# The skip term of a Mamba stack: u scaled by D in place on VectorE and added by TensorE transposes, instead of products with a diagonal matrix

## What is computed

```python
u = jax.nn.silu(jnp.transpose(xc, (0, 2, 1)))          # after the short convolution
dbl = u @ W_x
delta = jax.nn.softplus(dt @ W_dt + b_dt)
def step(h, inp):
    u_t, d_t, B_t, C_t = inp
    h = jnp.exp(d_t[..., None] * A) * h + (d_t * u_t)[..., None] * B_t[:, None, :]
    y = jnp.einsum('bds,bs->bd', h, C_t)
    return (h, y)
y = jnp.moveaxis(ys, 0, 1) + u * Dp                    # the skip term
y = y * jax.nn.silu(res)
return y @ W_out
```

## Time and profile before

| | |
|---|---|
| median of 3 runs | 2191.8 us (2189.04 to 2195.35) |
| profiled execution, its own time | 2192.7 us |
| its span, first to last instruction | 2190.9 us |
| TensorE busy | 94% of the span |
| VectorE, ScalarE, GpSimd busy | 68%, 66%, 68% |
| mean granted TensorE clock | 0.977 |

### The profile page before, as it was taken

How to read it: one execution, slowest core, us unless ns; L and a number is a source line. 1 busy time by engine, 2 the same in 40 slices (tenths; PEclk the granted TensorE clock), 3 DMA queues, 4 the chain that set the end, 5 groups by cost and what they waited for, 6 DMA issues and landing times.

```text
span 2190.9 us, 30857 instructions
## 1 busy us (share of the span) xinstructions
PE 2052.0 (94%) x11952; PEld 1444.5 (66%) x11952; DVE 1500.5 (68%) x1507; ACT 1450.1 (66%) x2294; POOL 1484.7 (68%) x845
## 2 busy tenths in 40 slices
PE   6989899999999999999999999999999889999997
PEld 3457677777777777777676777777777764444443
DVE  1268888888897989797879888887888970111201
ACT  0278888898887888888878888888788731000000
POOL 0039897989898888989897979798889960000000
PEclk9989999999999999999999999999999999989999
DMA  5211111111111112111111121111111410000000
GB/s 182 88 58 40 58 41 60 40 60 49 60 39 59 39 60 68 41 68 39 61 41 58 41 68 40 60 42 66 40 50 39 155 59 37 1 29 0 10 0 19
DMA packets 34137, 113.13 MB, mean 52 GB/s; under 512 B 6148, under 2 KB 8836, under 8 KB 33480
## 3 DMA queue, kind: packets, MB, share of 16 engines
q1 hardware_dynamic: 33992, 111.17, 14.9%
HBM read 95.95 MB, written 15.20 MB: 51 GB/s over the span
## 4 chain that ended last, share of the span: by engine, by line
PE 55%; DVE 15%; ACT 14%; issue 11%; POOL 4%; DMA 1%; SPq 0%; DVEq 0%; POOLq 0%; ACTq 0%
PE b_ps L1107 11%; PE y_all L1118 9%; DVE hid L855 8%; ACT hid L545 6%; ACT dub_t L558 5%; PE y_all L1216 5%; PE b_ps L1216 4%; DVE u L730 4%; PE bank_b L999 3%; POOL hid L418 3%; PE bank_a L1014 3%; PE y_all L919 3%; PE bank_b L1014 2%; PE bank_a L1023 2%; PE y_all L1229 2%
## 5 line engine op out<-in xcount | busy, mean ns | idle before, releaser
L855 DVE TENSOR_TENSOR_SCAN hid<-hid,b_ps 128x512 f32<-128x512 f32 x1024 | 1213.5, 1209 | 247.6 <-PE b_ps L1107 225.9
L418 POOL TENSOR_TENSOR hid<-hid,c_rep 128x1024 f32<-128x1024 f32 x512 | 1208.3, 2388 | 200.1 <-DVE hid L855 200.1
L1107 PEld LDWEIGHTS b_ps<-ident,dub_t 128*128 128x128 f32 x4096 | 481.8, 143 | 389.3 <-issue 220.1
L1107 PE MATMUL b_ps<-ident,dub_t 128*128 128x128 f32 x4096 | 637.8, 279 | 71.2 <-DVE hid L855 67.1
L545 ACT ACTIVATE hid<-delta,neg_a 128x512 f32<-128x512 f32 x1024 | 652.9, 711 | 0.4
L1118 PE MATMUL y_all<-ident,hid 128*128 128x128 f32 x4096 | 619.9, 275 | 7.3 <-POOL hid L418 6.3
L558 ACT ACTIVATE dub_t<-du_t,b_t 128x512 f32<-128x512 f32 x768 | 490.3, 712 | 58.9 <-PE b_ps L1107 57.2
L1118 PEld LDWEIGHTS y_all<-ident,hid 128*128 128x128 f32 x4096 | 484.1, 142 | 11.1 <-POOL hid L418 11.1
L409 POOL TENSOR_SCALAR dub_t<-du_t,b_t 128x512 f32<-128x512 f32 x256 | 174.7, 710 | 0.0
L730 DVE SCALAR_TENSOR_TENSOR u<-bank_b,conv_w_sb,u 128x511 f32<-128x511 f32 (+2 forms) x192 | 139.3, 725 | 0.7
L999 PE MATMUL bank_b<-xn,w_in_sb 128*128 128x512 f32 x256 | 132.1, 602 | 3.3 <-DVE u L730 3.3
(11 more groups left out here) (190 smaller groups left out, 1783.2 us busy)
## 6 DMA issues: line engine op xcount, KB each, us to landing
c_rep<-bc_dram SPq DMA_DIRECT2D x128, 512.0 KB, 3.7
hid<-x_t SPq DMA_DIRECT2D x4, 2048.0 KB, 8.7
x_dram<-x_out SPq DMA_DIRECT2D x16, 512.0 KB, 2.9
xt<-x_dram SPq DMA_DIRECT2D x15, 512.0 KB, 3.7
h_dram<-hid SPq DMA_DIRECT2D x4, 512.0 KB, 3.3
out<-y_d SPq DMA_DIRECT2D x4, 512.0 KB, 2.6
x_dram<-hid SPq DMA_DIRECT2D x3, 512.0 KB, 2.7
c_rep<-x_dram SPq DMA_DIRECT2D x3, 512.0 KB, 5.1
```

What stands on the lines that cost most here:

```text
L418: nc.gpsimd.tensor_tensor(part, part, c_rep[:, n % 2, s % GROUP, :].unsqueeze(1) .broadcast_to([P, HALF, SEQ]), ALU.mult).then_inc(hc_read ...
L855: nc.vector.tensor_tensor_scan(hid[:, i % RING, d, :], hid[:, i % RING, d, :], b_ps[d % 2][:, :], 0.0, ALU.mult, ALU.add)\
L1107: last = nc.tensor.transpose(b_ps[d % 2][:, c * P:(c + 1) * P], dub_t[:, i % DUB, c, d * P:(d + 1) * P], ident[:, :])
```

## The change

VectorE no longer makes diagonal matrices. In each step it multiplies block d of `u` by D in place (`scale_u`), at the slots of the new table `SCALE_U_AT`, after the scan of that slot. TensorE waits for that and adds the block with four transposes, in the form that `sum_states` has. Two of the four places in `SKIP_AT` move to later slots, and the two waits on `setup` go from 6 to 2.

```diff
-            diag_skip = sb("diag_skip", [P, NI, P])
+            scaled_u = sem("scaled_u")
...
-                    act.wait_ge(setup, 6)
+                    act.wait_ge(setup, 2)
...
-                    dve.wait_ge(ident_ready, 2)
-                    for d in range(NI):
-                        nc.vector.tensor_scalar(diag_skip[:, d, :], ident[:, :], vec_sb[:, 2, d:d + 1], None, ALU.mult)\
-                            .then_inc(setup, 1)
...
+                    def scale_u(k, d):
+                        dve.wait_ge(du_ready, 2 * k + d // HALF + 1)
+                        nc.vector.tensor_scalar(u[:, k % 2, d, :], u[:, k % 2, d, :], vec_sb[:, 2, d:d + 1], None, ALU.mult)\
+                            .then_inc(scaled_u, 1)
+
+                    SCALE_U_AT = {(3, 0): 0, (3, 1): 1, (3, 2): 2, (4, 1): 3}
...
+                                if live(k) and at in SCALE_U_AT:
+                                    scale_u(k, SCALE_U_AT[at])
...
                     def skip(k, d):
+                        pe.wait_ge(scaled_u, NI * k + d + 1)
                         for c in range(TC):
                             last = nc.tensor.matmul(y_ps[d][:, c * P:(c + 1) * P], u[:, k % 2, d, c * P:(c + 1) * P],
-                                                    diag_skip[:, d, :], start=False, stop=False, skip_group_check=True)
+                                                    ident[:, :], start=False, stop=False, is_transpose=True, skip_group_check=True)
                         last.then_inc(skip_done, 1)
...
-                    SKIP_AT = {(2, 1): 0, (2, 2): 1, (10, 0): 2, (10, 2): 3}
+                    SKIP_AT = {(5, 2): 0, (7, 3): 1, (10, 0): 2, (10, 2): 3}
...
-                                    pe.wait_ge(setup, 6)
+                                    pe.wait_ge(setup, 2)
```

## The result

| | before | changed |
|---|---|---|
| median | 2191.5 us (4 runs, 2189.0 to 2195.4) | 2223.6 us (4 runs, 2219.1 to 2230.9) |
| ratio to before | | 1.0148, 95% interval 1.0117 to 1.0180 |
| profiled execution, its span | 2192.7, 2190.9 us | 2224.2, 2222.4 us |
| mean granted TensorE clock | 0.977 | 0.964 |

The change costs 32 us. The forecast was 16, inside its range and on its side, but three quarters of the cost have a cause that the sum put at nothing: TensorE's clock. Ratios and intervals leave out executions more than 1.5% above the fastest of their kernel, three in experiment 1 and one in experiment 9.

What follows compares the result with a forecast made beforehand. The prediction took no single engine as the bound: the chain of waits changes engines a dozen times a step. Its terms, 6.2 + 4.9 + 1.3 + 4.5 - 0.8 = +16.1 us on 2192.7, gave about 2208, range 2187 to 2240.

Steps and rivals of the forecast that it cites:

- the 28.8 us taken from TensorE: 64 skip blocks, each 0.45 us shorter as transposes than as products; predicted to gain nothing, lying ahead of waits or under taps.
- The rival that TensorE's time counts: TensorE is the real bound, so its saved time is won: about 2163 us, or 2178 for half; chance 0.15.
- The block at (5, 2): Skip block moved into the stretch TensorE holds without a gap: +0.44 us per step, 6.2 us over steps 0 to 13.
- the cover: TensorE's 0.62 us wait for `y_copy` at (8, 2) was to absorb the 0.44 us block at (7, 3), costing nothing.
- The scalings against GpSimd: Scalings at (3, 0) to (4, 1) wait for running GpSimd products: 0.6 us each, 1.5 or more at (3, 2).
- a TensorE stall of 0.35 us: The late scan of (3, 3) was to hold up TensorE 0.35 us a step, 4.9 us over 14 steps.
- The rival of the lost races: GpSimd goes first at (3, 1) or (4, 1), stalling TensorE: 24 to 57 us, 2232 to 2265; chance 0.14.
- the rival that the scalings do not touch GpSimd: Scalings run without waiting for GpSimd, so the sum is +7.4 us: 2200 us; chance 0.2.
- Steps 14 and 15, and the diagonals: Step 14 +1.3 us on GpSimd, step 15 +4.5 on VectorE's scalings; no diagonals before the first step, -0.8.
- The clock: TensorE's slow stretches behind row sums and 16-column turns: one more or fewer, 5 us each side, nothing in the sum.
- the 1.8 us taken out of (2, 1) and (2, 2): Two skip blocks leave ahead of TensorE's wait for `gate` at (2, 3); the wait grows by 1.8 us, gain nothing.
- The rival of more slow stretches: Fewer products with weights let every step get a slow stretch: 13 more by 5.2 us, about 2275; chance 0.02.

Runs made afterwards that it cites:

- experiment 1: The changed kernel with its four skip blocks at (7, 3), (10, 0), (10, 2), (10, 3): 2217.1 us, ratio 1.0067 from its seven shortest runs of ten.
- experiment 9: The changed kernel with the row sums of squares taking 64 columns of ones instead of one: 2189.1 us, ratio 0.9982.
- experiment 4: The changed kernel without the scalings and TensorE's wait for them, so the factor D is left out: 2226.5 us, ratio 1.0147.
- experiment 5: The changed kernel with blocks 0 and 1 again as diagonal products at (2, 1) and (2, 2), only blocks 2 and 3 scaled: 2194.2 us, ratio 1.0006.
- experiment 6: experiment 1 plus eight faint products (1e-20 diagonal) at (2, 1) and (2, 2): 2196.4 us, ratio 1.0021.
- experiment 7: experiment 1 plus sixteen transposes of a faint 128x128 matrix at (2, 1) and (2, 2): 2195.0 us, ratio 1.0015.
- 12: experiment 1 with the row sums of squares taking 64 columns of ones instead of one: 2184.3 us, ratio 0.9959.
- experiments 3: The kernel before with two of block 1's four skip products moved from (2, 2) to (5, 2), no scalings: 2205.8 us, ratio 1.0058.
- 10: The changed kernel plus eight faint products (1e-20 diagonal) at (2, 1) and (2, 2): 2215.8 us, ratio 1.0097.
- experiment 8: The kernel before with the row sums of squares taking 64 columns of ones instead of one: 2176.1 us, ratio 0.9919.

## Why the prediction was right or wrong

**The bound, and the side.** Right. The chain changes engines often; the 28.8 us taken from TensorE bought nothing. The rival that TensorE's time counts fell at once: no step is below 102.5 us.

**The block at (5, 2).** Right to the hundredth. It was to add 0.44 us to every step, 6.2 in all; undisturbed steps are 0.45 us longer, 5.9 in all, and experiment 1 takes it away by moving the block. At (7, 3) the cover held: the wait for `y_copy` behind it shrank from 0.62 us to

```profile
1044.37 0.33 PE L1082 MATMUL bank_a<-ident,yg_t 128*128 128x128 f32 x1 [0.19 <-ACT y_d L527]
```

**The scalings against GpSimd.** The mechanism was right, the price was not. A one-input scaling does wait for a running GpSimd product, with the pattern of lengths worked out: short, short, long, slightly long (0.46, 0.46, 1.23 and 0.60 us). What the Trainium skill says (SBUF — State Buffer, Who interferes with whom), that a float32 `tensor_scalar` within SBUF and GpSimd lock each other out for whole instructions, the trace bears out with 1.23 us against 0.46. But the step that made a TensorE stall of 0.35 us of it, 4.9 us in all, failed: a free scaling is 0.46 us instead of 0.6, the waiting one 1.23 instead of 1.5 or more, and the two banks of `b_ps` took up what was left, a scan that starts 0.56 us later and is ready just in time. The stall did not occur, and by experiment 4 the scalings cost nothing in the steps. The rival of the lost races put its 24 to 57 us on a sum that held 4.9 of the same stall already; no scaling in an undisturbed step came near its 3 us. For the steps the rival that the scalings do not touch GpSimd had the right number for the wrong reason.

**Steps 14 and 15, and the diagonals.** 1.3 + 4.5 us were to come behind the last `dbl` copy; 2.8 did. Two of the four scalings of the last step waited, in the timeline of VectorE:

```profile
1739.26 1.89 DVE L744 TENSOR_SCALAR u<-u,vec_sb 128x512 f32<-128x512 f32 x1
...
1743.71 1.45 DVE L744 TENSOR_SCALAR u<-u,vec_sb 128x512 f32<-128x512 f32 x1
...
1753.47 1.61 DVE L761 TENSOR_TENSOR xt<-xt,xn 128x1024 f32<-128x1024 f32 x1
```

The last of these rows is the addition that took 5.80 us in the earlier trace rows: it now starts 1.9 us into the run of two GpSimd products instead of with it, and 4.2 us came back where the working had allowed for a part. That the place made the difference is argued, not tried. The comparison on eight columns, 4.32 us in the earlier trace rows, lost some of it again:

```profile
1792.22 6.76 DVE L786 TENSOR_TENSOR top<-logit 128x8 f32<-128x8 f32 x1
```

Both times it ends with a group of four GpSimd products (1767.4 before, 1798.95 after), and now it started earlier in it. The four scalings are 4.3 us together; 4.3 - 4.2 + 2.4 is 2.5 of the 2.8 us. So the scalings' own cost, 4.3 us here and 4.4 by experiment 4, was near the forecast's 5.8 for the two steps, and the sum missed what two other instructions would then wait less or more. Ahead of the first copy 1.7 us went, of which the diagonals' 0.8 is the part that was worked out; the rest, like the 4.4 us of the start-up, can be the clock there, and was not tried.

**The clock.** This is the step that failed. It was put as one slow stretch more or fewer, 5.2 us each (4.5 measured), and at nothing in the sum. It was 24 us, three quarters of the result: 19.9 in seven slow steps instead of three, 4.4 in the start-up, which may be chance. Two sentences of the prediction stood close to it. One costed the 1.8 us taken out of (2, 1) and (2, 2) at nothing, since the wait behind them takes them up. Their direct cost was nothing (experiment 5 against 1: the same undisturbed step), though what grew was less the wait for `gate` than two new ones for scans. But they were what kept TensorE fed at a place where it then waits, and without them that place starts slow stretches of its own (experiments 1, 6, 7, 12). The other saw that "small shifts" decide which step gets a stretch at the squares, and took them as noise. They are not only that. With the place full and steps of 102.98 us there are three long stretches, three or four steps apart (before, experiments 5, 6 and 7); with steps 0.45 us longer there are four and five, two or three steps apart (experiments 3 and 10); and widening the squares removed them all (experiments 8 and 9). How the length of a step sets that spacing, the runs don't show, and two lengths are too few for a rule. The rival of more slow stretches named the right effect with a chance of 0.02, and dismissed it by the earlier trace rows.

That dismissal was right in what it said. By the page's rule in the Trainium skill (TensorE: Matmul & The Clock Gate, PE-mode transpose) the 16 idle transposes of experiment 7 should have done nothing for the clock; they did the same as the products of experiment 6, 2195.0 against 2196.4 us. Transposes were not the trouble. Fewer microseconds of work were, and it made no difference which of these two kinds filled them. The kind did matter at the squares, where one-column products hold TensorE as long as wide ones and left its clock at 1.2 GHz behind them in three steps (experiment 8).

**The number.** Against 2192.7, the terms as measured in the two profiled executions are 5.9 for the steps (6.2 forecast), 0 for the stall (4.9), 2.8 behind the last copy (5.8), -1.7 ahead of the first (-0.8), and 24 for the clock (0): +31, where the forecast had +16. That the forecast lies in the right half of its range is in part luck: 8 us of terms that did not come stood in for clock that did, and the range reached to 2240 for lost races, of which there were none.

## What to carry to other kernels

Before taking work off TensorE ahead of a wait, look where its slow stretches begin and what the edit leaves at such places: an engine's time that "costs nothing" may be what keeps its clock up, and here 1.8 us a step were worth 8 us (intervals touching) in the changed kernel and 12 to 21 in experiment 1. Where a profile shows slow stretches behind a group of one-column products, widen them first; it costs no time and was worth 0.8% here, more than any move of work. And give a time that hangs on the pattern of slow stretches a wide range, since steps longer by 0.45 us in 103, with TensorE's work in place, took them from three to four and five, and an emptied place of 1.8 us to eight.

## What the runs showed of the hardware

- One-column products hold TensorE for as long as wide ones do: eight float32 products in 1.70 us with one column, eight in 1.74 with 64. With one column slow stretches of 10.2 us followed in three steps, with 64 in none between 150 and 1700 us.
- Slow stretches can chain: in experiment 1 a short one and a long one alternated over six steps, 109.2 us each instead of 102.98, and the same program took 2197 to 2248 us.
- Two 128x128 float32 transposes take the time of one product of that size: eight in 0.88 us here, four products in 0.89.
- A two-input addition of VectorE in the last step took 1.61 us in the changed kernel, 3.46 in experiment 4, 3.43 in experiment 8 and 5.80 in the kernel before, the same instruction each time beside GpSimd products; which moment against them gives which time was not tried.
